# Softmax sums inverted before or after they are spread over the head's columns

## The reference

```
h = concatenate([clip(sum |conv(x)|, 0, 1), table[x_txt]], axis=1)     # 16 x 333 x 256
h = h + attn(layernorm(h))        # 16 heads of 16, windows of 128 with stride 64, plus one for the last 128
h = h + experts(layernorm(h))     # top 2 of 8 experts, hidden width 512, weighted by the gate's softmax
```

## Time and profile before

| | |
|---|---|
| times of three runs | 1410.8, 1412.46, 1412.97 us (median 1412.46) |
| the profiled execution | 1410.24 us, of it the span of instructions 1408.4 us |
| mean granted TensorE clock | 0.923 of full speed |
| busy: TensorE, VectorE, ScalarE, GpSimd | 1183.9, 983.4, 784.0, 611.2 us |
| an image in the middle (401.70 to 450.30) | 48.60 us |
| the reciprocals L767 | 80 of 1748 ns, 139.8 us busy |

### The profile page before, as it was taken

How to read it: one execution, slowest core, us unless ns; L and a number is a source line. 1 busy time by engine, 2 the same in 40 slices (tenths; PEclk the granted TensorE clock), 3 DMA queues, 4 the chain that set the end, 5 groups by cost and what they waited for, 6 DMA issues and landing times.

```text
span 1408.4 us, 34891 instructions
## 1 busy us (share of the span) xinstructions
PE 1183.9 (84%) x10190; PEld 950.9 (68%) x10191; DVE 983.4 (70%) x4131; ACT 784.0 (56%) x3176; POOL 611.2 (43%) x900
## 2 busy tenths in 40 slices
PE   2376788889888887888888783799999999999996
PEld 1254565556556655665555552799999999999995
DVE  4495999999999999989999885344444444444442
ACT  0195898888889898988988990111111111111110
POOL 5333456456556645664663434122323223223232
PEclk9697899989999999988998986899999999999998
DMA  3694653464356346435633606233232322322322
GB/s 109 131 240 91 107 118 88 98 136 99 84 114 128 89 91 132 105 81 111 140 80 73 114 31 210 50 50 49 45 48 49 48 45 48 49 46 47 49 48 32
DMA packets 98402, 123.35 MB, mean 88 GB/s; under 512 B 15545, under 2 KB 87417, under 8 KB 95193
## 3 DMA queue, kind: packets, MB, share of 16 engines
q1 hardware_dynamic: 75880, 89.96, 30.4%
q0 software_dynamic: 18576, 24.47, 10.8%
q10 hardware_dynamic: 3808, 7.34, 1.7%
HBM read 69.35 MB, written 46.07 MB: 82 GB/s over the span
## 4 chain that ended last, share of the span: by engine, by line
PE 57%; DVE 9%; issue 9%; DMA 8%; ACT 7%; POOL 7%; SPq 3%; POOLq 0%; DVEq 0%; ACTq 0%
PE s_bank L1163 12%; PE t_bank L1163 12%; PE o_bank L1178 11%; PE t_bank L1035 5%; ACT probs L621 5%; PE m_bank L1099 5%; DMA qk_parts<-parts_flat 3%; PE o_bank L1058 3%; PE s_bank L1021 3%; DVE probs L756 2%; DMA stacks<-qk_parts 2%; DMA expert_slots<-rows,slot_i 2%; PE m_bank L999 2%; POOL expert_slots L492 2%; PE m_bank L1152 1%
## 5 line engine op out<-in xcount | busy, mean ns | idle before, releaser
L621 ACT ACTIVATE probs<-probs,neg_max 128x128 f32<-128x128 f32 x1280 | 496.5, 398 | 22.2 <-DVE neg_max L756 21.7
L756 DVE CUSTOM_DVE_ANT_0 probs<-s_bank,nbias 128x128 f32<-128x128 f32 x1280 | 292.2, 284 | 47.8 <-PE s_bank L1021 46.7
L621 ACT ACTIVATION_READ_ACCUMULATOR probs<-probs,neg_max 128x1 f32 x1280 | 254.0, 198 | 0.0
L1035 PE MATMUL t_bank<-ident,probs 128*128 128x128 f32 x1280 | 217.8, 297 | 38.6 <-ACT probs L621 38.4
L680 ACT ACTIVATE v_all<-s_bank 128x512 f32<-128x512 f32 x91 | 54.4, 598 | 286.5 <-PE s_bank L1163 266.4
L1058 PE MATMUL o_bank<-probsT,v_all 128*32 128x128 f32 x2560 | 146.1, 303 | 55.3 <-issue 29.8
L1021 PE MATMUL s_bank<-stacks 96*128 96x128 bf16 x1280 | 137.9, 235 | 57.8 <-DMA stacks<-qk_parts 44.3
L1035 PEld LDWEIGHTS t_bank<-ident,probs 128*128 128x128 f32 x1280 | 150.4, 153 | 50.3 <-ACT probs L621 49.3
L635 ACT ACTIVATE probsT<-t_bank 128x512 f32<-128x512 f32 x240 | 141.8, 591 | 71.0 <-PE t_bank L1035 69.6
L1021 PEld LDWEIGHTS s_bank<-stacks 96*128 96x128 bf16 x1280 | 94.4, 105 | 122.5 <-DMA stacks<-qk_parts 47.9
L1178 PE MATMUL o_bank<-stacks,v_all 128*128 x728 | 172.6, 380 | 0.8 <-issue 0.7
(11 more groups left out here) (157 smaller groups left out, 2091.0 us busy)
## 6 DMA issues: line engine op xcount, KB each, us to landing
stacks<-qk_parts SPq DMA_DIRECT2D x192, 166.5 KB
qk_parts<-parts_flat SPq DMA_DIRECT2D x192, 83.2 KB
nbias<-expert_slots SPq DMA_DIRECT2D x91, 129.0 KB
w_sb<-in_L_ffn_w_dram ACTq DMA_DIRECT2D x14, 512.0 KB
v_all<-v_all SPq DMA_DIRECT2D x64, 96.0 KB, 6.6
x_here<-in_x_dram SPq DMA_DIRECT2D x16, 256.0 KB, 5.9
out_dram<-h_res SPq DMA_DIRECT2D x16, 256.0 KB
stacks<-in_L_ffn_w_dram SPq DMA_DIRECT2D x8, 512.0 KB
```

The source lines that it names most:

```text
L621: ins = act.activation(seg, seg, ACT.Exp, bias=neg_max[:, r, i:i + 1], scale=-1.0, accum_out=row_sum[:, (par + v) % 2, h:h + 1])
L756: ins = dve.tensor_tensor_reduce(probs[:, r, i * WIN:(i + 1) * WIN], s_bank[:, k % 2, i * WIN:(i + 1) * WIN], nbias[:, h, :], 1.0, BIG, AL ...
L1035: mm = pe.transpose(t_bank[:, (k - 3) % 2, i * WIN:(i + 1) * WIN], probs[:, r, i * WIN:(i + 1) * WIN], ident[:, :])
```

## The change

VectorE now takes the reciprocal over the sixteen sums only, into `inv_sum`. The spreading over 256 columns is a copy on GpSimd with a broadcast input, which raises `weight_ready`. A new semaphore `inv_ready` tells GpSimd, and tells ScalarE that a buffer of sums may be written again. The wait for the transposes of two windows before (`weightT_done`) moves to GpSimd, and VectorE waits for the copy of two windows before. The copy is written at the top of steps 2, 6, 10, 14 and 18, one step after the reciprocal's step.

```diff
+        inv_ready = sem("inv_ready")
 ...
                 for k in range(G):                       # GpSimd
+                    v = (k - 3) // NG
+                    if (k - 3) % NG == 3 and ((att and v >= 0) or (tail and v < 0)):
+                        wv, vp = b * NW + v, (par + v) % 2
+                        pool.wait_ge(inv_ready, wv + 1)
+                        if wv >= 2:
+                            pool.wait_ge(weightT_done, wv - 1)
+                        pool.tensor_copy(weight[:, vp, :, :], inv_sum[:, vp, :].unsqueeze(2).to_broadcast([P, H, HD]))\
+                            .then_inc(weight_ready, 1)
 ...
                         if g == 0 and b * NW + v >= 2:   # ScalarE
-                            act.wait_ge(weight_ready, b * NW + v - 1)
+                            act.wait_ge(inv_ready, b * NW + v - 1)
 ...
                         dve.wait_ge(exp_ready, n + 1)    # VectorE
                         if wv >= 2:
-                            dve.wait_ge(weightT_done, wv - 1)
-                        dve.reciprocal(weight[:, vp, :, :], row_sum[:, vp, :].unsqueeze(2).to_broadcast([P, H, HD]))\
-                            .then_inc(weight_ready, 1)
+                            dve.wait_ge(weight_ready, wv - 1)
+                        dve.reciprocal(inv_sum[:, vp, :], row_sum[:, vp, :]).then_inc(inv_ready, 1)
```

## The result

The changed kernel takes 1434.7 us (median of 4 runs, 1432.3 to 1439.0) against 1411.8 for the kernel before (4 runs). The ratio is 1.0165, interval 1.0139 to 1.0191: slower by 1.65%, some 23 us. The profiled execution is the slowest of the four, 1439.04 us with a span of 1437.3, so profile against profile shows 28.8 us.

What follows compares the result with a forecast made beforehand. An image was taken as a chain that changes engine, VectorE the bound by share alone. Per image 0.5 + 1.3 + 0.4 = +2.2 us, over 13 images +28.6, less 4.5: 1434.3, forecast 1436 us at the median; range 1400 to 1456.

Steps and rivals of the forecast that it cites:

- The reciprocal: VectorE's reciprocal over 16 columns takes 257 ns instead of 1748, giving back 119 us of VectorE time in all.
- stretch (b): Steps 9 to 15, to head_out of the third window: two reciprocals, 3.0 us; VectorE ends 1.46 us after ScalarE.
- The copy of w1: Second window's GpSimd copy, step 10, queued behind scatters and split: ends at 441.6, TensorE waits 3 us for the weights.
- The clock: Low TensorE clock over the v projection after the weights wait: 1.3 us an image, range 0.5 to 2.2.
- xn: Last step of an image: GpSimd keeps what it shares with VectorE through copy and h_res; xn ends 0.4 us later.
- my two outcomes: For xn beside GpSimd's copy and h_res: ends 0.4 us later, or VectorE gets in and it ends 1.07 earlier.
- the images without a full GpSimd row: Images 0, 1 and 15 and the last window, outside images 2 to 14: give back 4.5 us together.
- Rival 1: Second window's weights are in time, so the stretch shrinks until ScalarE binds: 1378 us, chance 0.13.
- Rival 2: TensorE's clock stays up after the idle: 1420 us, chance 0.18.
- Rival 3: VectorE gets the shared port pair after the copy, at xn: 1418 us, 1401 with the clock up; chance 0.12.
- Rival 4: GpSimd copy takes 0.82 us or is held up by VectorE's additions, adding 0.4 in three windows: 1453 us, chance 0.15.
- first xn near 2.3 us: Sign that the forecast is right: the first of the three xn instructions on VectorE takes about 2.3 us.

Runs made afterwards that it cites:

- e1: The changed kernel with the GpSimd copy for the second window moved to step 9, ahead of the last split: 1396.8 us, ratio 0.9867.
- e4: The kernel before, wide reciprocal kept, plus five GpSimd broadcast copies an image that nobody reads or waits for: 1419.6 us, ratio 1.0029.
- e8: The changed kernel with the second window's copy one step later, behind GpSimd's fourteen-instruction root of step 11: 1495.2 us, ratio 1.057.
- e3: The changed kernel with 26 unread transposes on TensorE ahead of its wait for the second window's weights, images 2 to 14: 1406.3 us, ratio 0.9934.
- e5: The kernel before, with GpSimd's h_res addition of step 18 made to wait until VectorE's three xn instructions are done: 1391.3 us, ratio 0.984.
- e2: The changed kernel with the spreading copy on VectorE, behind its probsT copy, instead of on GpSimd: 1402.0 us, ratio 0.9903.

## Why the prediction was right

The forecast was 1436, the time 1434.7. Step by step:

**The reciprocal.** 257 ns forecast, 249 measured. VectorE's 119 us came out as 102.5 of busy time. Other instructions grew, the last casts L746 by 7.7 us in all (753 ns in the mean against 511) and the probsT copies by 3.2 (672 against 632), while anti fell by 9.8 (715 against 1323); these don't add up to the difference, and I haven't assigned the rest. Off the chain they were worth nothing, as said; in stretch (b) the saving was 1.63 us, forecast 1.5. head_out of w2 starts 0.09 us after ScalarE's weightT of w2 ends (415.72 and 415.63), in place of 1.46: the stretch is now as long as ScalarE's work in it.

**The copy of w1.** Forecast near 441.6, 2.0 later than TensorE used to take it; measured 1.99 in the mean, and a TensorE wait of 3.27 us (forecast 3). e1, e4 and e8 show that it is the place and not the copy: earlier TensorE does not wait, later the wait grows one to one, and copies that nobody waits for cost 0.3% in all. The bare copy is 0.40, as interpolated. Here it took 0.94 because VectorE's diag addition with two inputs ran from 401.37 too:

```profile
401.37 0.93 POOL L517 COPY weight<-inv_sum 128x256 f32<-128x256 f32 x1
...
401.37 0.69 DVE L873 TENSOR_TENSOR diag<-diag,anti 128x512 f32<-128x512 f32 x1
```

In the two images where the w1 copy is 0.41, TensorE waited 2.74 instead of 3.27; the 0.53 is this meeting. I had named it, and left it out of the sum. By the rule of the Trainium skill (SBUF — State Buffer, § Who interferes with whom) a VectorE instruction with two SBUF inputs contends with a GpSimd instruction that reads SBUF. The trace agrees: the copy ends 0.24 us after the addition, and in the image where it started 0.17 ahead of the addition (503.73) it took 0.41, and the addition 0.80.

**The clock.** The term was right in kind and 0.7 us an image too small: 2.05 against 1.3. I had taken the middle between all and nothing, on the ground that the low stretch might miss the work. It never missed: the idle and the work behind it come in the same order every image, and the mean over eleven is near the end that I called "all in it" (1.9 plus 0.5). Taking the middle was a guess. e3 took the whole term away.

**xn.** Here the working failed. The forecast was that GpSimd keeps the pair through copy and h_res and xn ends 0.4 later. The rows of xn's line in one image (ns min/median/max) say something else:

```profile
L722 DVE TENSOR_SCALAR xn<-h_in,moments,rstd x3: 401/453/1931, 420.9 to 423.1; 128x256 f32<-128x256 f32 x3
```

and so does VectorE's timeline there:

```profile
420.91 2.63 DVE L722 TENSOR_SCALAR xn<-h_in,moments,rstd 128x256 f32<-128x256 f32 x3 [1.47 <-POOL rstd L484]
```

The first xn took 0.45 beside the copy (0.40, from 420.82), and the second, begun after h_res (421.17), took 1.93. From head_out of w2 to the end of xn are 7.82 us, against 7.74 before. So neither of my two outcomes, but a third: one instruction passes and the next is caught. The row of anti, on which I had leaned, was no match for this case: a GpSimd scatter ran from 382.01 to 383.00 ahead of the split, which I hadn't named, and behind a copy it came out otherwise. xn's end moved by 0.1, not 0.4. That error and the clock's nearly cancel, +0.7 and -0.3, and that is luck.

**Sum.** +2.44 an image against +2.2. Times 13 that is 31.7, and the profile has 28.8, so the images without a full GpSimd row gave back 2.9, forecast 4.5. (At the h_res near 162 us, ahead of the 13 images, the changed kernel was 3.0 ahead, 161.67 against 164.71.) The mechanism held, w1's wait with the clock behind it. That 1436 came within 1.3 us of 1434.7 is in part luck: the sum was worked from one profiled execution to another and had 24.1 us, where these two differ by 28.8 and the medians by 22.9.

**Rivals.** Rival 1, weights in time, is what e1 makes of the kernel, but its gain was priced too high: 1378 forecast, 1397 measured. Its sum has no term for the low clock behind h_res, which in e1 lasts 6.8 to 9.8 us. Its decisive point held: whether w1's copy comes before or after TensorE's arrival. Rival 2 (clock stays up) was put at 1420; e3, which is that case, is at 1406, so I had underrated the term there as well. Rival 3 fell by the timeline: one xn did get in beside the copy, but xn as a whole ended no earlier. Rival 4 (dear copy) held in part: 0.51 in the mean and 0.94 for w1.

Slips in the prediction: the transposes that release ScalarE in (b) are those of group 9, made in step 12, not of step 9; and TensorE's 3 us were written as "2.0 more than it lost before", which is the 0.97 of the earlier trace rows plus the 2.0; head_out of w2 "to about 453.5" can't come before the weightT that it needs, put at 453.6; and the sign "first xn near 2.3 us" did not come: the first took 0.45 and the second 1.93.

## What to carry to other kernels

Work that goes to an engine with idle time is hidden only if that engine gets to it in time: read, in program order, what it still has to do at the step where the result is asked for, not its share of busy time. Where a new wait leaves TensorE idle, look for two prices, the wait and what the idle does to the clock; here each was some 2 us an image. And where two engines block each other on one pair of instructions, one extra wait that orders them (e5, 1.6%) can be worth more than making an instruction of the busiest engine seven times shorter (e1 1.3%, with the copy well placed).

## What the runs showed of the hardware

- Transposes that nobody reads (26, 3.06 us) in an idle of TensorE saved 28 to 33 us in the whole, by the clock: granted 1.00 in the work behind, against 0.50 without them (e3).
- An idle of 7.20 us costs no more of the clock than one of 3.27 (4.90 against 4.93 us to the next probsT, e8).
- A VectorE copy of 128x256 with a broadcast input took 284 ns in the median and up to 1885 beside GpSimd (e2); GpSimd's own took 398 ns in the median (390 to 941, changed kernel).
- A VectorE tensor_scalar begun 0.09 us into a GpSimd copy of 0.40 us passed beside it (0.45 us, against 0.40 alone), while its successor, begun 0.1 us into the next GpSimd instruction, was held for the rest of it (1.93 us).
